# Attention on TensorE of one Trainium2 core: scores beside raw tiles in the two halves of the array, value products in two parts of 256 columns

## The reference

```
scores = einsum('bhqd,bhkd->bhqk', Q, K) / 4        # layer 0 adds -0.1 |t_k - t_q|
attn   = softmax(scores, axis=-1)
out    = einsum('bhqk,bhkd->bhqd', attn, V)
```

## Time and profile before

| | us |
|---|---|
| median of 3 runs | 1030.07 (1028.42 to 1044.67) |
| the profiled execution, own time | 1031.82 |
| its span in the profile | 1030.0 |
| mean granted clock of PE | 0.904 |
| PE busy | 858.3 (83%) |
| DVE busy | 585.8 (57%) |
| ACT busy | 428.8 (42%) |

### The profile page before, as it was taken

The page is one execution under the profiler, slowest core; times in us unless marked ns, Lnnn a source line. Parts: engine busy times, 40 slices in busy tenths (PEclk is TensorE's granted clock), DMA queues, the critical chain, the costliest instruction groups (busy, mean ns, idle before and its releaser), DMA issues. The chain is left out here.

```text
span 1030.0 us, 11821 instructions
## 1 busy us (share of the span) xinstructions
PE 858.3 (83%) x4356; PEld 499.8 (49%) x4356; DVE 585.8 (57%) x938; ACT 428.8 (42%) x813; POOL 239.9 (23%) x269
## 2 busy tenths in 40 slices
PE   3953888888888989954988888889399999999994
PEld 2621333333325669821333333322267877878774
DVE  2825777777714845725777777760870503433226
ACT  1220566666674366420466565674421021021110
POOL 1100344444442367400000000010511022011121
PEclk9985799999999999985599899995599999998998
DMA  9644222222104300054722121200000000000000
GB/s 226 198 133 153 63 63 63 64 63 64 33 2 136 92 18 2 1 144 144 251 62 65 41 64 53 63 2 0 2 1 0 2 0 21 1 1 21 1 21 21
DMA packets 39626, 60.67 MB, mean 59 GB/s; under 512 B 7112, under 2 KB 17096, under 8 KB 39312
## 3 DMA queue, kind: packets, MB, share of 16 engines
q1 hardware_dynamic: 38704, 58.99, 19.8%
q0 software_dynamic: 864, 0.92, 0.6%
HBM read 40.02 MB, written 18.87 MB: 57 GB/s over the span
## 5 line engine op out<-in xcount | busy, mean ns | idle before, releaser
L981 DVE TENSOR_REDUCE row_max<-ps_wide 128x2 f32<-128x1024 f32 x256 | 302.2, 1224 | 84.4 <-PE ps_wide L422 84.4
L710 ACT ACTIVATE probs<-ps_a 128x512 f32<-128x512 f32 x342 | 192.7, 598 | 103.5 <-PE ps_a L448 73.3
L422 PE MATMUL ps_wide<-stack_k,stack_q 48*128 48x512 f32 x512 | 153.3, 489 | 60.4 <-DVE planes L956 44.5
L448 PE MATMUL ps_a<-stack_q,stack_k 62*128 62x512 f32 (+1 forms) x342 | 145.5, 504 | 19.1 <-ACT probs L710 18.7
L458 PE MATMUL ps_out<-probs,vals 128*32 128x512 f32 x1024 | 147.9, 653 | 14.8 <-ACT out_rows L702 14.4
L448 PEld LDWEIGHTS ps_a<-stack_q,stack_k 62*128 62x128 f32 (+1 forms) x342 | 58.1, 199 | 135.4 <-ACT probs L710 90.8
L710 ACT ACTIVATE probs<-ps_misc 128x512 f32<-128x512 f32 x170 | 101.8, 599 | 46.2 <-PE ps_a L448 29.1
L802 ACT ACTIVATE hid_full<-ps_a 128x512 f32<-128x512 f32 x32 | 19.1, 598 | 220.9 <-PE ps_a L626 159.3
L848 POOL TENSOR_TENSOR probs<-probs,fixes_sb 128x512 f32<-128x512 f32 x64 | 81.7, 1277 | 108.5 <-ACT probs L710 108.5
L422 PEld LDWEIGHTS ps_wide<-stack_k,stack_q 48*128 48x128 f32 x512 | 62.5, 209 | 79.9 <-DVE planes L956 46.1
L448 PE MATMUL ps_misc<-stack_q,stack_k 62*128 62x512 f32 (+1 forms) x170 | 85.2, 501 | 9.3 <-ACT probs L710 9.3
(11 more groups left out here) (137 smaller groups left out, 1233.9 us busy)
## 6 DMA issues: line engine op xcount, KB each, us to landing
planes_k<-planes SPq DMA_DIRECT2D x32, 256.0 KB, 3.8
planes_q<-planes SPq DMA_DIRECT2D x32, 256.0 KB, 4.0
stack_q<-planes_q SPq DMA_DIRECT2D x64, 128.0 KB, 2.8
stack_k<-planes_k SPq DMA_DIRECT2D x64, 128.0 KB, 2.8
stack_q<-planes_q SPq DMA_DIRECT2D x64, 64.0 KB, 2.6
stack_k<-planes_k SPq DMA_DIRECT2D x64, 64.0 KB, 2.5
w_e_raw<-in_L_W SPq DMA_DIRECT2D x1, 4096.0 KB, 12.8
ctxT<-in_ctxT SPq DMA_DIRECT2D x1, 2048.0 KB, 13.9
```

What stands on the lines that cost most here:

```text
L422: mm(item_slot(("pair", g, p))[:, i * S:(i + 1) * S], stack_q[at, slot(g, c) + q * P:slot(g, c) + (q + 1) * P], stack_k[at, slot(g, c):slo ...
L448: mm(tiles_x[n % 3][:], stack_k[at, slot(g, c) + k * P:slot(g, c) + (k + 1) * P], stack_q[at, slot(g, c):slot(g, c) + S], start=True, stop ...
L710: do(probs[n % PROBS][:, j, :], tiles_x[(n * HG + j) % 3][:], ACT.Exp, scale=0.25).then_inc(exp_done, 1)
L981: v.tensor_reduce(row_max[:, g % 2, :, p], item_slot(("pair", g, p))[:].rearrange("p (i k) -> p i k", i=2), AX, ALU.max).then_inc(max_done, 1)
```

## The change

`scores` and `for_maximum` issue one of their two matmuls a call. In a half k tile PE now issues the score of the lower half, the raw tile of the upper half, the score of the upper half and the raw tile of the lower half. `weigh` takes a part: after each half k tile it issues the four value products of 256 of the 512 columns. The wait for the probabilities and, at the first k tile of a group, for `out_kept` stand before part 0. `turns` follows the second half tile of k = 1. ACT's two waits on `pv_done` count twice as many.

```diff
-                def for_maximum(g, p):
+                def for_maximum(g, p, i, first):
...
-                    if p == 0:
+                    if p == 0 and first:
                         pe.wait_ge(sem(f"stack_loaded{l}_{g % RING}"), 16 * LOADS * (g // RING + 1))
-                    slot_free(("pair", g, p))
-                    for i in range(2):
...
+                    if first:
+                        slot_free(("pair", g, p))
...
-                def scores(g, k, c):
+                def scores(g, k, c, i):
...
-                def weigh(n):
+                def weigh(n, part):
...
+                    if part == 0:
+                        pe.wait_ge(probs_ready, n + 1 if l == 0 else HG * (n + 1))
+                    if part == 0 and k == 0:
+                        wait(pe, sem(f"out_kept{l}"), g)
+                    cols = slice(part * S // 2, (part + 1) * S // 2)
+                    for j in range(HG):
+                        mm(po[32 * j:32 * j + VW, cols], vals[:, k, g * HG + j, :], probs[n % PROBS][:, j, cols],
+                           start=(k == 0 and part == 0), stop=(k == QT - 1), skip_group_check=True).then_inc(sem(f"pv_done{l}"), 1)
...
                     for k in range(QT):
                         for c in range(2):
-                            scores(g, k, c)
-                            if ahead < G:
-                                for_maximum(ahead, 2 * k + c)
-                        if k == 1:
-                            turns(ahead)
-                        if g * QT + k >= BEHIND:
-                            weigh(g * QT + k - BEHIND)
+                            for i in range(2):
+                                scores(g, k, c, i)
+                                if ahead < G:
+                                    for_maximum(ahead, 2 * k + c, 1 - i, i == 0)
+                            if k == 1 and c == 1:
+                                turns(ahead)
+                            weigh(g * QT + k - BEHIND, c)
                 for n in range(G * QT - BEHIND, G * QT):
-                    weigh(n)
+                    for part in range(2):
+                        weigh(n, part)
...
-                    act.wait_ge(pv_done, QT * HG * (g + 1))
+                    act.wait_ge(pv_done, 2 * QT * HG * (g + 1))
...
-                        act.wait_ge(pv_done, HG * (n - PROBS + 1))
+                        act.wait_ge(pv_done, 2 * HG * (n - PROBS + 1))
```

More of the change, by code:

```diff
@@ L412, in slot_free @@
                             pe.wait_ge(normalised, past[1] - BEHIND - 1)
-                def for_maximum(g, p):
+                def for_maximum(g, p, i, first):
                     c, q = divmod(p, QT)
-                    if p == 0:
+                    if p == 0 and first:
                         pe.wait_ge(sem(f"stack_loaded{l}_{g % RING}"), 16 * LOADS * (g // RING + 1))
-                    slot_free(("pair", g, p))
-                    for i in range(2):
-                        at = slice(HALF * i, HALF * i + KS)
-                        mm(item_slot(("pair", g, p))[:, i * S:(i + 1) * S], stack_q[at, slot(g, c) + q * P:slot(g, c) + (q + 1) * P],
-                           stack_k[at, slot(g, c):slot(g, c) + S], start=True, stop=True).then_inc(raw_done, 1)
+                    if first:
+                        slot_free(("pair", g, p))
+                    at = slice(HALF * i, HALF * i + KS)
+                    mm(item_slot(("pair", g, p))[:, i * S:(i + 1) * S], stack_q[at, slot(g, c) + q * P:slot(g, c) + (q + 1) * P],
+                       stack_k[at, slot(g, c):slot(g, c) + S], start=True, stop=True).then_inc(raw_done, 1)
                 def turns(g):
@@ L438, in turns @@
                         last.then_inc(sem(f"out_turned{l}"), 1)
-                def scores(g, k, c):
-                    if k == 0 and c == 0:
+                def scores(g, k, c, i):
+                    if k == 0 and c == 0 and i == 0:
                         pe.wait_ge(sem(f"max_sent{l}_{g % 2}"), 32 * (g // 2 + 1))
-                    for i in range(2):
[L445 to L449, removed]
@@ L451, in weigh @@
-                def weigh(n):
[L453 to L462, removed]
+                    n = (g * QT + k) * HG + 2 * c + i
@@ new lines, in scores @@
+                    wait(pe, exp_done, n - 2)
+                    at = slice(HALF * i, HALF * i + rows)
+                    mm(tiles_x[n % 3][:], stack_k[at, slot(g, c) + k * P:slot(g, c) + (k + 1) * P],
+                       stack_q[at, slot(g, c):slot(g, c) + S], start=True, stop=True).then_inc(scores_done, 1)
+                def weigh(n, part):
+                    if n < 0:
+                        return
+                    g, k = divmod(n, QT)
+                    if part == 0:
[6 more added lines that the diff above has]
+                           start=(k == 0 and part == 0), stop=(k == QT - 1), skip_group_check=True).then_inc(sem(f"pv_done{l}"), 1)
@@ L463, in attention @@
+                for p in range(PAIRS):
+                    for i in range(2):
+                        for_maximum(0, p, i, i == 0)
                 for p in range(PAIRS):
@@ L465, in attention @@
                         turns(1)
-                    for_maximum(1, p)
+                    for i in range(2):
+                        for_maximum(1, p, i, i == 0)
                 pe.wait_ge(sem(f"rows_in{l}"), 16 * (N_ATT if l == 0 else 2))
```

## The result

The changed kernel takes 1103.88 us (median of 4 runs, 1098.3 to 1122.02) against 1029.72 us for the kernel before in the same comparison: a ratio of 1.071, with a 95% interval of 1.065 to 1.076. It is slower by 7%. The forecast was 1100 us.

The account below looks back on a forecast made before the run. PE's own order was taken as the bound, 12.80 us a group. Twelve low intervals + 85.2, fourteen high - 5.2, layer 1's existing losses - 8, last groups - 2: + 70, giving 1100 us against the median; range 1008 to 1200.

Parts of the forecast that it names:

- the moved wait: Tile k = 2: products ask for ACT's output copy at T + 0.66, still leave at T + 2.39; PE idles 1.65 us.
- High-clock group: Attention loops at 2.4 GHz: four k tiles of 4.19, 2.46, 2.46 and 3.32 make 12.43 us a group, against 12.80.
- Low-clock group: Attention loops at 1.2 GHz: 5.84 + 2 x 4.30 + 5.48 = 19.9 us a group, 7.1 more than 12.80.
- If nothing else happens: Whole kernel without clock falls: 14 us saved, 1018 us in the profiled execution, 1016 against the median.
- Rival A: Both attention loops: the clock holds at 1.00 despite the gaps, 1016 us; chance 0.20.
- A fall at every second or third gap: Attention loops: the 1.65 us idle stretch in each group lowers the granted clock at every second or third occurrence.
- 12 of 26 intervals low: Group intervals at half clock: three in layer 0, nine in layer 1, each 7.1 us longer, 85.2 us in all.
- returns should not be quicker: Attention loops: returns to 1.00 came behind undivided products; with these halved, the clock should come back no sooner.
- Rival B: Both attention loops: the clock never comes back, for want of unbroken products; + 172 us, 1200 us; chance 0.12.
- Rival C: Halved value products: the clock holds but emptying the array makes each cost 0.71 us; + 29 on A, 1045; chance 0.07.
- Rival D: Tile k = 2: ACT's output copy doesn't bind; group 10.7 us, 971 us in all; chance 0.04.

Follow-up runs that it names:

- the filled gap: Changed kernel with PE repeating eight unread value products before the products that wait for the output copy at k = 2: 1016.26 us, ratio 0.980 against the kernel before.
- the early copy: ACT's output copy moved ahead of tile k = 2's first exponential: on the changed kernel 974.34 us; with only the halved products, scores and raw tiles in old order, 972.3.

## Why the prediction was right, point by point

The forecast of 1100 us met 1103.88, and its mechanism is the one that the runs show: the moved wait, the idle stretch and the fall of the clock. How many groups would be low was a guess, and there the total owes something to luck, as the fourth point says.

- **High-clock group.** 12.43 us was worked out; 12.45 is what the changed kernel shows between the starts of L431 at 200.69 and 213.14, at the high clock, and the filled one in all groups from 152.7 to 277.2. Its terms: half tile 1.23 (1.24 measured), product of 256 columns 0.57 (0.57), products at T + 2.39 (2.38), idle 1.65 (1.63). The 0.32 in the half tile is 0.33 by the prediction's own times, which changes nothing.
- **Low-clock group.** Half tile 2.15: two product starts lie 2.16 apart (617.55 and 619.71, below), and their product takes 1.01 as written. The one group that was low throughout, written as 19.9, came as 20.9, with DVE's variance in it (610.5 to 631.4).

```profile
617.55 1.08 PE L461 MATMUL ps_out<-probs,vals 128*32 128x256 f32 x8
618.56 0.79 PE L447 MATMUL ps_misc<-stack_q,stack_k 50*128 50x512 f32 x1
...
619.71 1.08 PE L461 MATMUL ps_out<-probs,vals 128*32 128x256 f32 x8
```

- **If nothing else happens**, 1016 us: the filled gap gave 1016.26. To the microsecond that is chance, as the kernel before was 9 us slower beside it (1038.53); the group of 12.45 us is the firmer agreement. Rival A was the right sum for a clock that holds, and failed on its condition. The Trainium skill, TensorE: Matmul & The Clock Gate, section Why this matters for your kernels, warns only of idle gaps longer than these; the trace does not agree, as gaps of 1.63 us once a group took the mean clock to 0.83 and 0.66.
- **A fall at every second or third gap** was somewhat too few for layer 0: from 118 to 290 us the granted clock fell seven times at eleven gaps of 1.2 us or more. The low intervals were wrong in kind and in place, and their cost was right in sum. The prediction had 12 of 26 intervals low throughout, 239 us at 19.9 each. The windows of the 13 intervals of either layer give about 175 us at the low clock:

```profile
128.65:312.21 183.56, 161.85 (x1302) 60.35 (x1302) 130.89 (x125) 120.61 (x235) 74.92 (x91) 0.85 0.18 50
542.67:756.00 213.33, 189.48 (x1301) 67.69 (x1301) 141.19 (x164) 120.93 (x234) 13.05 (x42) 0.72 0.15 43
```

  That time is spread over 20 intervals, and one alone is low throughout. Three intervals in layer 0 and nine in layer 1 were to cost 18 and 54 us; the layers lost 28 and 39. That 72 meets 67 is luck in part: too little in layer 0, too much in layer 1. Layer 0's first groups, which begin at the low clock, took 16.0 and 15.0 us between starts (112.6, 128.6, 143.6) where they had taken 12.9 and 12.4; the sum had given them nothing.
- **The step that failed** is "after the change the longest such piece is half, so returns should not be quicker". Low stretches in layer 0 were as short as 3.3 us (160.5 to 163.8), and the kernel with whole products and the gap had less high clock in layer 1 (0.60 against 0.66) and stayed low for up to 75 us on end, against 37. What brings the clock back is not the unbroken product; what does is not shown. Rival B stood on this and fell with it.
- **Rival C**, a dearer product part, is out by the 0.57 in the timeline. **Rival D**, the copy not binding, is out by the 1.63; made true by the early copy, its 971 us came out at 972 to 974, though its group of 10.7 us came out at 11.0 and the kernel before was slower beside these runs, so the agreement of the totals is partly chance.
- Not foreseen: the gap alone, with whole products, left the clock of layer 0 up.

## What to carry to other kernels

When a consumer is cut finer and moved earlier, list what its first instruction waits for and who makes that ready in which place of its own queue: here two lines on ACT had to move with PE's order. Sum such a wait twice, once as time and once as idleness of TensorE; in a loop where PE is neither full nor idle, the moved wait cost 20 us as time (996.24 to 1016.26) and some 90 as a lower clock. If the producer can't come earlier, a few repeated products that nobody reads are a remedy and a test in one.

## What the runs showed of the hardware that was not expected

- Repeating value products (1.5 us a group) made the kernel 88 us faster, and four of 256 columns were nearly as good (84 us).
- With the halved products, the line between harmless and harmful idle stretches lay between 1.07 and 1.63 us in layer 0, once in 12.5 us. It is no property of the gap alone: 1.65 us in each group of layer 0, with whole products, left the clock at 1.00 from 126 to 311 us, and 1.60 us between the layers did nothing.
- In the low stretches of layer 0 from 118 to 290 us PE is never idle (10.10 of 10.10 us busy in the longest), and yet the low stretches behind the seven falls last 3.3 to 10.1 us, and in layer 1 up to 37 us, from 597.5 to 634.8:

```profile
597.50:634.80 37.30, 35.76 (x192) 12.52 (x190) 22.95 (x32) 17.27 (x33) 1.70 (x6) 0.50 0.16 44
```
